# Casting the first expert's matrices beside the attention, and loading the first head's weights uncast

## The reference

```python
x = layernorm(x + attn(x))        # 4 heads of 256
x = layernorm(x + ffn(x))

# attn: q, k, v = silu(causal_conv4(x @ W.T)); beta, gamma, mix = sigmoid(x @ Wb.T / Wdec.T / Wmix.T)
# o_d   = gated delta rule over chunks, S <- S + k^T u, u = T(beta v) - T(beta k) S, with l2-normed q, k
# ema   = running mean of v by gamma
# o     = rmsnorm((1 - mix) * o_d + mix * ema) @ Wo.T

# ffn: 8 experts, each takes the 512 tokens that score highest for it
probs = softmax(x @ choice_w.T); G, I = top_k(probs.T, 512)
out[I] += G * (silu(x[I] @ w1[e]) @ w2[e])      # w1[e] 1024 x 2048, w2[e] 2048 x 1024, e = 0..7
```

## Time and profile before

| | us |
|---|---|
| three runs | 1205.19, 1205.75, 1208.89 (median 1205.75) |
| profiled execution, its own time | 1209.13 |
| its span on the slowest core (core 0) | 1207.5 |
| spans of the eight cores | 1198.2 to 1207.5 |

### The profile page before, as it was taken

How to read it: one execution, slowest core, us unless ns; L and a number is a source line. 1 busy time by engine, 2 the same in 40 slices (tenths; PEclk the granted TensorE clock), 3 DMA queues, 4 the chain that set the end, 5 groups by cost and what they waited for, 6 DMA issues and landing times.

```text
span 1207.5 us, 23424 instructions; the slowest of 8 cores (1198.2 to 1207.5 us)
## 1 busy us (share of the span) xinstructions
PE 1027.0 (85%) x7432; PEld 573.9 (48%) x7559; DVE 541.1 (45%) x1202; ACT 532.3 (44%) x967; POOL 329.0 (27%) x493
## 2 busy tenths in 40 slices
PE   1888999799989999989960179999999999999992
PEld 0455565466656666655530144444444444444441
DVE  3256666766676666667645512212121212100173
ACT  1356666566666666658861032222222222222253
POOL 2012323533353333222230102313131313131035
PEclk9899999899999999999985579999999999999997
DMA  9965597965586555333799919998989898988595
GB/s 195 138 140 104 142 164 169 166 153 140 141 150 165 135 138 135 101 106 141 225 249 213 174 48 156 208 196 184 198 197 193 196 188 187 194 194 221 194 361 211
DMA packets 106468, 208.66 MB, mean 173 GB/s; under 512 B 8055, under 2 KB 56183, under 8 KB 106352
## 3 DMA queue, kind: packets, MB, share of 16 engines
q0 software_dynamic: 70608, 110.89, 54.9%
q1 hardware_dynamic: 35744, 96.27, 23.9%
HBM read 219.50 MB, written 67.11 MB: 237 GB/s over the span
## 4 chain that ended last, share of the span: by engine, by line
PE 73%; DMA 7%; DVE 6%; issue 6%; ACT 3%; POOL 2%; SPq 1%; DVEq 0%; POOLq 0%; ACTq 0%
PE ps L1367 16%; PE ps L1388 16%; PE ps L503 14%; PE ps L550 4%; PE ps L1036 3%; PE ps L587 2%; DMA AR<-accd 2%; PE ps L766 2%; PE ps L778 2%; DMA AR<-hs 2%; PE ps L859 2%; PE ps L768 1%; DMA AR<-x1s,idxc 1%; PE ps L863 1%; DVE AR L1235 1%
## 5 line engine op out<-in xcount | busy, mean ns | idle before, releaser
L1367 PE MATMUL ps<-AR 128*128 128x512 bf16 x993 | 230.8, 380 | 14.3 <-ACT AR L1459 11.5
L1388 PE MATMUL ps<-AR 128*128 128x512 bf16 x969 | 218.6, 380 | 1.2
L503 PE MATMUL ps<-AR 128*128 128x512 bf16 x724 | 174.2, 387 | 8.2 <-DVE gt L481 4.2
L1388 PEld LDWEIGHTS ps<-AR 128*128 128x128 bf16 x992 | 95.9, 98 | 111.6 <-issue 3.5
L1475 ACT ACTIVATE AR<-ps 128x512 bf16<-128x512 f32 x128 | 76.1, 597 | 159.1 <-PE ps L1367 159.1
L1367 PEld LDWEIGHTS ps<-AR 128*128 128x128 bf16 x1024 | 92.8, 97 | 111.7 <-issue 14.4
L1459 ACT ACTIVATE AR<-ps 128x1024 bf16<-128x1024 bf16 x32 | 32.4, 1025 | 242.3 <-PE ps L1315 242.3
L503 PEld LDWEIGHTS ps<-AR 128*128 128x128 bf16 x768 | 74.3, 100 | 83.0 <-issue 12.4
L821 ACT ACTIVATE AR<-ps 128x512 bf16<-128x512 f32 x160 | 86.7, 597 | 29.2 <-PE ps L768 29.2
L1425 DVE TENSOR_SCALAR AR<-ps,gcol 128x512 f32<-128x512 f32 x48 | 33.8, 747 | 144.9 <-PE ps L1388 144.9
L539 DVE CAST AR<-ps 128x512 bf16<-128x512 f32 x96 | 66.6, 693 | 57.0 <-PE ps L503 54.6
...
...
## 6 DMA issues: line engine op xcount, KB each, us to landing
AR<-w POOLq DMA_DIRECT2D x36, 1024.0 KB, 21.9
AR<-w POOLq DMA_DIRECT2D x56, 512.0 KB, 7.2
w<-AR SPq DMA_DIRECT2D x56, 512.0 KB, 3.4
AR<-w SPq DMA_DIRECT2D x28, 1024.0 KB, 16.8
AR<-hs SPq DMA_DIRECT2D x16, 512.0 KB, 6.1
accd<-AR SPq DMA_DIRECT2D x16, 512.0 KB, 4.1
AR<-accd SPq DMA_DIRECT2D x16, 512.0 KB, 12.1
...
```

The source lines that it names most:

```text
L503: mm = T.matmul(ps[:, 0:512], w[:, kk, 128 * (i % 2):128 * (i % 2 + 1)], g.hs_fm[b][:, 512 * kk:512 * (kk + 1)], start=(kk == 0), stop=(kk ...
L1367: mm = T.matmul(ps[:, 0:512], w1[:, kk, 128 * (m % 4):128 * (m % 4 + 1)], xe[:, KTOP * kk:KTOP * (kk + 1)], start=(kk == 0), stop=(kk == 7))
L1388: mm = T.matmul(pss[nh][:, 0:512], g.h_fm[kk][:, 128 * tm:128 * (tm + 1)], w2[:, kk % 4, 512 * nh:512 * (nh + 1)], start=(kk == 0), stop=( ...
```

## The change

1. `NPC` goes from 56 to 72: the eight first chunks are w1 of expert 0 (into a new `w116`), the other 64 are w2 of all eight experts. Five chunks a unit, at t1, t3, t5, t7 and t8. There are four bounce buffers for chunks 20 to 59 (units 4 to 11), the two new ones in the late part of `ofm`; chunks 0 to 19 and 60 to 71 go through two.
2. w1 and w2 of expert 0 are loaded plain from the copies, still on POOL's queue. w1's pieces 0 and 1 are issued after tile 14, pieces 2 and 3 and w2's 0 to 2 after tile 15. w1's pieces 4 and 5 belong to expert 1 and are still cast.
3. Head 0's wk, wq and wv all come by SP in float32 (wq and wv into the space of `wos`). VectorE casts all of wk and wv, ScalarE all of wq. SP issues the small weights and c1 first. POOL waits for wk before its loads of hs.
4. VectorE makes the diagonals of head 0 ahead of its casts; those of head 1 move to POOL, unit 1, step t2.

```diff
-NPC = 56
+NPC = 72
@@ dve_cast, act_cast
     V.wait_ge(g.d_k0.sem, g.d_k0.at())
-    V.tensor_copy(out=g.wt[1][:, 0:1024], in_=g.st_wk[:, 0:1024]).then_inc(g.v_st.sem, g.v_st.up("wk"))
+    V.tensor_copy(out=g.wt[1], in_=g.st_wk).then_inc(g.v_st.sem, g.v_st.up("wk"))
+def dve_cast_v(g, V):
+    V.wait_ge(g.d_v0.sem, g.d_v0.at())
+    V.tensor_copy(out=g.wt[2], in_=g.wos.bitcast(F32)[:, 2048:4096]).then_inc(g.v_st.sem, g.v_st.up("wv"))
...
-    A.wait_ge(g.d_k0.sem, g.d_k0.at())
-    A.activation(out=g.wt[1][:, 1024:2048], in_=g.st_wk[:, 1024:2048],
+    A.wait_ge(g.d_q0.sem, g.d_q0.at())
+    A.activation(out=g.wt[0], in_=g.wos.bitcast(F32)[:, 0:2048], func=AF.Copy).then_inc(g.a_st.sem, g.a_st.up("wq"))
@@ pool_early
-    if t == 10:
+    if t == NT - 2:
+        P.wait_ge(g.d_res[(NT - 1) % 6].sem, g.d_res[(NT - 1) % 6].at(NT - 1))
         P.wait_ge(g.pe_V.sem, g.pe_V.at(NU - 1, 1))
...
-    if 10 <= t < 14:
-        load_w1(g, P, t - 10)
+        load_w1(g, P, 0)
+        load_w1(g, P, 1)
     if t == NT - 1:
+        for Q in (2, 3):
+            load_w1(g, P, Q)
         for Q in range(3):
-            load_w2(g, P, Q, g.w2)
+            load_w2(g, P, Q, g.w216)
@@ dve_program
-    dve_cast(g, V)
     V.wait_ge(g.d_sm.sem, g.d_sm.at())
     V.wait_ge(g.d_c1.sem, g.d_c1.at())
-    for h in range(2):
-        diag(g, V, h)
+    diag(g, V, 0)
+    dve_cast(g, V)
@@ bounce buffers
+def bounce(x):
+    return x % 4 if 20 <= x < 60 else x % 2
 def pool_cast(g, P, x):
-    if x >= 2:
-        P.wait_ge(g.d_bs[x % 2].sem, g.d_bs[x % 2].at(x - 2))
+    i = bounce(x)
+    y = last_before(x, i)
+    if y is not None:
+        P.wait_ge(g.d_bs[i].sem, g.d_bs[i].at(y))
...
@@ pool_program
-    P.wait_ge(g.d_hs[0].sem, g.d_hs[0].at())
-    pool_weights(g, P, 0)
+    P.wait_ge(g.d_k0.sem, g.d_k0.at())
...
-            if k % 2 == 1 and 4 * n < NPC:
-                pool_cast(g, P, 4 * n + k // 2)
-            if k == 2 and n in (5, 9):
+            if k in (1, 3, 5, 7, 8) and 5 * n + k // 2 < NPC:
+                pool_cast(g, P, 5 * n + k // 2)
+            if k == 2 and n in (1, 5, 9):
                 diag(g, P, n // 4 + 1)
```

More of the change, by code:

```diff
@@ L179, in build_once @@
     late = g.ofm[:, 12288:16384]
+    g.d["bnc"] += cols(late, 2048, 2)
     g.d["st_hs"], g.d["st_wk"] = g.ofm[:, 0:8192].bitcast(F32), g.ofm[:, 8192:12288].bitcast(F32)
@@ L1019, in act_ot @@
     A.wait_ge(g.pe_ot.sem, g.pe_ot.at(n, ct))
+    if (n, ct) == (12, 0):
+        for i in (2, 3):
+            A.wait_ge(g.d_bs[i].sem, g.d_bs[i].at(last_before(NPC, i)))
     A.activation(out=g.ofm.rearrange("p (f t) -> p f t", f=8)[:, 2 * h + ct, 512 * b:512 * (b + 1)],
@@ L1148, in sp_out @@
     Y.wait_ge(g.pe_V.sem, g.pe_V.at(NU - 1, 1))
-    for i in range(2):
-        Y.wait_ge(g.d_bs[i].sem, g.d_bs[i].at(NPC - 2 + i))
+    for i in range(4):
+        Y.wait_ge(g.d_bs[i].sem, g.d_bs[i].at(last_before(NPC, i)))
     for t in range(6):
@@ L1810, in pool_weights @@
         P.wait_ge(g.pe_P.sem, g.pe_P.at(4 * (h - 2) + 3, 5))
-    for k in (1, 0, 2) if h > 0 else (0, 2):
+    for k in (1, 0, 2):
         i = 3 * (h % 2) + k
@@ L1821, in pool_hs, with chunk_of, last_before @@
                 ).then_inc(g.d_hs[b].sem, g.d_hs[b].up())
-def chunk_of(w, x):
-    e, j = 1 + x // 8, x % 8
-    return w[e][256 * j:256 * (j + 1), :].rearrange("(p r) m -> p (r m)", r=2)
-def pool_cast(g, P, x):
-    if x >= 2:
-        P.wait_ge(g.d_bs[x % 2].sem, g.d_bs[x % 2].at(x - 2))
-    P.dma_start(out=g.bnc[x % 2], in_=chunk_of(g.w2, x)).then_inc(g.d_bl[x % 2].sem, g.d_bl[x % 2].up(x))
+def chunk_of(w1, w2, x):
+    if x < 8:
+        return w1[128 * x:128 * (x + 1), :]
+    e, j = divmod(x - 8, 8)
+    return w2[e][256 * j:256 * (j + 1), :].rearrange("(p r) m -> p (r m)", r=2)
+def bounce(x):
+    return x % 4 if 20 <= x < 60 else x % 2
+def last_before(x, i):
+    return max((y for y in range(x) if bounce(y) == i), default=None)
+def pool_cast(g, P, x):
+    i = bounce(x)
+    y = last_before(x, i)
+    if y is not None:
+        P.wait_ge(g.d_bs[i].sem, g.d_bs[i].at(y))
+    elif i >= 2:
+        P.wait_ge(g.v_G.sem, g.v_G.at(3))
+        P.wait_ge(g.pe_GT.sem, g.pe_GT.at(3))
+    P.dma_start(out=g.bnc[i], in_=chunk_of(g.w1[0], g.w2, x)).then_inc(g.d_bl[i].sem, g.d_bl[i].up(x))
 def pool_wo(g, P):
+    P.wait_ge(g.v_st.sem, g.v_st.at("wv"))
+    P.wait_ge(g.a_st.sem, g.a_st.at("wq"))
     P.dma_start(out=g.wos.rearrange("p (kk m) -> p kk m", kk=8),
```

35 lines of the change are left out of this document (20 added, 15 removed).

## The result

The changed kernel takes 1215.34 us (median of five runs, 1214.00 to 1218.54) against 1206.82 for the kernel before in the same session (1205.19 to 1209.67). The ratio is 1.0074, 95% interval 1.0050 to 1.0098: slower by some 9 us. The forecast was 1201, and the range ended at 1211.

A forecast was written before the change was run, and what follows sets the result against it. TensorE carries nearly all of the chain of waits, besides two long DMA pieces (a residual tile, the first gather). Terms -6.3 - 10.5 + 1 + 2 + 9 = -4.8 us took the median from 1205.75 to 1201; range 1190 to 1211.

The forecast's parts named there:

- a: Row tiles: with w1's loads moved behind tile 14, the last add follows TensorE's product; -6.3 us.
- b: First gather of token rows: eight of ten loads become plain, so the gather finds empty DMA engines; -10.5 us.
- Term e: Five chunks a unit: in unit 3 POOL's fifth chunk waits for a store and makes rkq late; +9 us.
- the rival of the slow rotation: Two-buffer rotation above 12.5 us makes POOL and rkq late in each of units 0 to 3; 1213 us, chance 0.12.
- Term d: Head 1's diagonals on POOL in unit 1 hold a scan of VectorE; +2 us, bounds 0 and 6.5.
- Term c: Start: ScalarE's cast of wq stands ahead of the first sigmoid, so TensorE's second product P comes later; +1 us.

The follow-up runs named there:

- e4: The kernel before with w1's first four loads issued after row tiles 14 and 15, still casting; 1209.95 us, ratio 1.0024.
- e6: The changed kernel with expert 0's w1 and w2 read from float32 and cast on the way again, at the same places; 1234.63 us, ratio 1.0224.
- e2: The changed kernel with Wo's casting load at the end of unit 3's steps instead of unit 2's; 1210.27 and 1213.67 us.
- e3: The changed kernel with head 1's diagonals made by VectorE at the start, not by POOL in unit 1; 1212.21 us, ratio 1.0037.
- e5: The changed kernel with each unit's fifth chunk issued behind the next unit's rkq and diagonals, Wo still behind unit 2's fifth chunk; 1201.83 us, ratio 0.9943.

## Why the prediction was wrong

**The gains were right.** a and b together: -16.7 us in the mean of the cores, -16.8 predicted. The split was off (a -3.9, b -12.8). For b, core 0, on which the prediction reckoned, stood at 21.8 us where the mean is 23.2; it is 10.8 there and 10.4 in the mean now, where 10.9 was predicted. For a, the row tiles gave 3.9 us where e4 gives 6.1; which part of the stretch behind the last rkq took the rest isn't known. b's reason held with less room than thought: the queue was empty 2.8 us ahead of the gather, not 6, since its first load came 2.2 us later than reckoned. The price of a plain load, 3.5, was about right. e4 and e6 show that b needs both parts of the change: late places alone cost 2.4 us, and casting loads at these places 20.6.

**Term e was the step that failed.** Its mechanism, POOL's fifth chunk waiting ahead of rkq in unit 3, is in the chain, the two waits and TensorE's idle time; its size, +9, was not right: the interval grew by 13.3 us in the mean. By the prediction's numbers, which are core 0's, it was to be 197.1 - 156.04 = 41.1 us. It is 42.6 on core 0, 44.9 in the mean, and 47.6 on cores 4 and 5. On core 4 the wait behind Wo ended 191.69 - 158.87 = 32.8 us after rkq 3, not 185.2 - 156.04 = 29.2: 3.6 more, of which 2.8 are Wo's own landing. With a chunk more ahead of it, it took 28.2 us instead of 22.4:

```profile
AR<-woT POOLq DMA_DIRECT2D x1, 2048.0 KB, 28.2
```

The next load and store and their issue took 203.38 - 191.69 = 11.7, not 9.5: 2.2 more. The operations ahead of rkq took 3.1, not 2.4. In sum 6.5. For the store I had used the page's median, 3.4. The trace of the kernel before has other numbers at this very place, for the store beside Wo (issued at 156.93) and for that of the chunk of 181.67:

```profile
w<-AR SPq DMA_DIRECT2D x1, 512.0 KB, 8.7
...
w<-AR SPq DMA_DIRECT2D x1, 512.0 KB, 6.2
```

With 6.2 for 3.4 the forecast interval is 43.9 us, near the mean of the cores. The DMA engines were 0.95 busy there before the change already (150 to 180 us), and 0.94 after it; the median is that of the whole kernel. The price was also set against TensorE being held 1.4 us less than VectorE (by the rows 5.86 - 4.54 = 1.3): it stood 3.52 + 10.38 us, and then ran at 0.63 of the clock.

**"From unit 4 on four buffers hide every wait; in units 12 to 14 two suffice" was wrong in both halves.** e2 shows the first: with Wo beside them four buffers leave a unit of 41.7 us. A rotation of 12.4 to 12.6 us shows the second, +2.1 us in the mean and up to 6.2 on core 4. That is the rival of the slow rotation, at its very threshold of 12.5 us, but in a place other than units 0 to 3, to which I had confined it. The "under 11 us" held against it took a load of 6.1 us from one row and a store of 3.4; the page's median for the loads was 7.2 already:

```profile
AR<-w POOLq DMA_DIRECT2D x56, 512.0 KB, 7.2
```

**Term d was half its size**: +4.1, of which 2.72 us are TensorE's wait and the rest lies in a stretch with the clock at 0.89. My upper bound of 6.5 had both, but I chose 2 since unit 1 "isn't so full". e3 takes it out alone; in e5, which leaves the products on POOL, the scan isn't held and the interval is 33.7, so the price is that of the held scan.

**Term c had the wrong sign and hardly mattered**: P began at 28.39, as predicted, but its two products took 4.95 us; -0.9 rather than +1 at the first rkq.

Summed: c, d and e were forecast at +12 and were +16.5; unit 13 and the small rest, forecast at nothing, add 3.9. That makes the mean span +3.7 instead of -4.8. The other 5 us, from the mean to the slowest core, I had left out: waits that come from DMA differ from core to core (rkq 3 to 4: 42.6 to 47.6 us, where before had 30.8 to 33.1), and the slowest core counts. In the profiled executions it stood 4.1 us above the mean before, and 9.4 after. This pair overstates it. In the five runs of the changed kernel the slowest core is 5.3 to 9.4 us above the mean, 7.2 on average, and in 46 runs of the kernel before, from the experiments' sessions, 4.7; the means over the cores are 1207.4 and 1201.3. So of the 8.5 us some 6 are in every core's time and some 2.5 in the spread.
